# Fused attention block on one core: TensorE multiplies zeros at the start and between the last steps, and the planner's opening times move forward

## The chip, the cores and the metric

The kernel runs on one core of a Trainium2 chip. The time is the device time in microseconds of one launch. The core's engines run side by side, each in the order of its own program: TensorE (PE in the rows, with PEld for its weight loads), VectorE (DVE), ScalarE (ACT), GpSimd (POOL) and SyncE (SP, which here issues most DMAs). They wait for each other by semaphores. TensorE's clock has two levels, 1.2 and 2.4 GHz; the profile calls the upper one 1.00 and the lower one 0.50.

## The reference, cut to what matters

One transformer block, post-norm, for 2048 tokens of width 128, 16 heads of 8, all in fp32:

```
qkv  = x @ W_qkv.T                      # 2048 x 384
q, k = rope(q), rope(k)
p    = softmax(causal(q @ k.T / sqrt(8)))
attn = (p @ v) @ W_o.T
x1   = layernorm(x + attn)
w    = int4_simulated(kernel)           # scale = max|kernel| / 7, round, clip
out  = layernorm(x1 + x1 @ w + bias + (x1 @ a) @ b)
```

## The kernel before, in words

The 2048 tokens are cut into four chunks of 512, the 16 heads into four groups of four. A task is one group on the queries of one chunk; causality means that chunk c needs the keys of chunks 0 to c. `ORDER` lists the sixteen pairs, the last one is split into two halves, so that there are 17 tasks, 0 to 16. Tasks 15 and 16 hold two tiles of 128 tokens each, the others four.

For each task TensorE does three kinds of work. "A" units are scores with queries on the partitions, of which VectorE takes row maxima (L1231 with its masks L1241 and L1245 on TensorE, L1052 on VectorE). "M" turns the maxima into rows (L1255), VectorE splits them in two parts (L1072, L1074), and GpSimd's DMAs put them beside the queries (L890), so that the maximum is subtracted inside the second product. "S" steps are the scores again, with keys on the partitions (L1275), ScalarE takes the exponentials (L974), GpSimd zeroes the upper triangle on diagonal blocks (L881). "PV" steps multiply by the values and by a column of ones (L1289), into one PSUM bank a task; ScalarE copies that bank out (L983), "O" transposes it to rows of tokens (L1298), VectorE divides by the sums (L1098, L1100).

Behind the last group of a chunk come its "POST" steps: 2 transposes the attention's output (L1315), ScalarE or VectorE copies it; 3 multiplies by W_o (L1317), VectorE adds x and takes the statistics (L1125, L1128, L1131); RSTD is on GpSimd (L853, L856), NORM on VectorE (L1140), BIAS on GpSimd (L861); 4 transposes again (L1319); 5 multiplies by the quantised weights (L1321); then statistics, RSTD and NORM once more, and the store. For the last three tasks ScalarE copies the results of 2 and 4 (L988).

The opening is a fixed list, `PROLOGUE`: P projects a chunk for q (0) or k (1), plain and with swapped pairs (L1199), into one of four banks in turn; VectorE multiplies by the cosine and sine table `cs` (L1022; for chunks 2 and 3 ScalarE copies and GpSimd multiplies, L897); R adds the two (L799, on VectorE for chunk 0, on GpSimd for the rest); H is ScalarE's rounding to the high part (L951), T the low part (L804, same engine as R); E selects the rows of group 0 by a multiply with a 0/1 matrix (L1215) and copies them; D stores the parts to DRAM; X transposes x of a chunk (L1188), V projects the values (L1205). Before that list TensorE transposes two weight blocks (L1174) and x of chunk 0 (L1188, copied by VectorE at L1013). GpSimd's program starts with memsets and casts (L808 to L848) and has its R and T steps behind them.

What sets the order of all this is a planner that runs when the kernel is built (`Course`, `schedule()`): a beam search over a model of the engines, with rough costs. Its clock starts at `BEGIN`, entries of `PROLOGUE` with a first number are not taken before that time, `IN_DRAM` says when each chunk's parts are in DRAM and the loads of later operands can begin, and the low-rank step L is due at a fixed 200.0. These numbers reach the chip only through the order that comes out, `SCHEDULE`: every engine walks the same list and issues its own part, with waits on semaphores, not on times. The planner also deals out the eight PSUM banks: `take` picks one, `give` says when it is free again, `HELD` keeps which event had which. The bank of a task's PV sums is given back when ScalarE has copied it out.

In that list the TensorE steps after O of task 16, the last task, are POST 2 of 16, 4 of 15, 3 of 16, 5 of 15, 4 of 16, 5 of 16; on VectorE the statistics of POST 5 of task 15 stand ahead of NORM 0 of task 16.

## Time and profile before

| | us |
|---|---|
| three runs | 441.98, 443.64, 443.79; median 443.64 |
| the profiled execution | 442.17 |
| its span (first to last instruction) | 440.4 |
| TensorE busy | 415.8 (94%) |
| VectorE busy | 379.3 (86%) |
| ScalarE busy | 317.4 (72%) |
| GpSimd busy | 119.3 (27%) |
| mean granted clock of TensorE | 0.984 |

A row of a timeline is: start in the span, duration, engine, line, operation, what is written and read, shape, how many instructions are merged, and in brackets how long the engine had been idle and what ended that. An fp32 multiply leaves two records on TensorE, a transpose one. A duration of several merged records runs from the first start to the last end, the drain of the last included, so that the next instruction on TensorE can begin before it is over. The column of the granted clock shows 1.00 until the trace has its first event of the clock.

### The profile page before, as it was taken

How to read it: one execution, taken by the hardware profiler on the slowest of the kernel's cores; microseconds unless marked ns; L12 is line 12 of the kernel's file. 1: busy time of each engine (PE TensorE's matmuls, PEld its weight loads, DVE VectorE, ACT ScalarE, POOL GpSimd, SP SyncE). 2: the span in 40 equal slices, each digit the busy share in tenths (PEclk: the TensorE clock that was granted, in tenths of full speed). 3: DMA queues.
4: the chain of work that ended last, by engine and by line, in shares of the span. 5: the costliest groups of instructions: out<-in, count | busy, mean ns of one | idle time of the engine just before them, and what ended most of it. 6: DMA issues, size and time to landing. Idle time of an engine off the chain costs nothing.

```text
span 440.4 us, 8586 instructions
## 1 busy us (share of the span) xinstructions
PE 415.8 (94%) x3246; PEld 205.3 (47%) x3246; DVE 379.3 (86%) x491; ACT 317.4 (72%) x643; POOL 119.3 (27%) x188
## 2 busy tenths in 40 slices
PE   5989899799999999999999999999999999999982
PEld 2546445344436353455443644444354454435651
DVE  2878799899999999999999999999987988585585
ACT  2454884386975687777888788878788878898760
POOL 8979602102113100223110322011003012225463
PEclk9999999799999999999999999999999999999996
DMA  7522322210000000022200022200000000000001
GB/s 241 177 97 90 111 81 71 56 30 3 2 0 2 4 1 3 1 80 63 61 3 0 2 66 77 60 3 0 2 1 2 1 3 2 3 25 2 1 26 48
DMA packets 12201, 16.58 MB, mean 38 GB/s; under 512 B 2444, under 2 KB 7324, under 8 KB 12160
## 3 DMA queue, kind: packets, MB, share of 16 engines
q1 hardware_dynamic: 11072, 15.75, 11.3%
q8 instruction: 26, 0.43, 0.4%
q0 software_dynamic: 1088, 0.28, 0.4%
q14 instruction: 15, 0.12, 0.1%
HBM read 10.37 MB, written 5.24 MB: 35 GB/s over the span
## 4 chain that ended last, share of the span: by engine, by line
PE 81%; DVE 8%; ACT 5%; issue 3%; POOL 1%; DMA 1%; POOLq 0%; DVEq 0%; ACTq 0%
PE ps L1289 28%; PE ps L1275 23%; PE ps L1231 17%; DVE pmax L1052 7%; ACT probs L974 4%; PE ps L1199 3%; PE ps L1298 2%; PE ps L1245 1%; PE ps L1241 1%; PE ps L1205 1%; PE ps L1255 1%; PE ps L1317 1%; POOL rstd L856 1%; PE ps L1215 1%; DMA wqkv_sb<-in_L_attn_W_qkv_dram 1%
## 5 line engine op out<-in xcount | busy, mean ns | idle before, releaser
L1052 DVE TENSOR_REDUCE pmax<-ps 128x2 f32<-128x1024 f32 (+3 forms) x273 | 319.2, 1216 | 34.5 <-PE ps L1231 18.7
L974 ACT ACTIVATE probs<-ps 128x512 f32<-128x512 f32 (+2 forms) x576 | 285.4, 583 | 78.1 <-PE ps L1275 76.6
L1275 PE MATMUL ps<-qS,kS 64*128 64x512 f32 (+3 forms) x664 | 163.8, 404 | 2.7 <-DVE pmax L1052 1.3
L1231 PE MATMUL ps<-kS,qS 64*128 64x512 f32 (+3 forms) x640 | 141.9, 414 | 5.5 <-DVE pmax L1052 2.4
L1289 PE MATMUL ps<-probs,vP 128*9 128x512 f32 (+3 forms) x1328 | 144.3, 520 | 0.2
L1275 PEld LDWEIGHTS ps<-qS,kS 64*128 64x128 f32 x664 | 84.5, 186 | 85.5 <-ACT probs L974 61.4
L1231 PEld LDWEIGHTS ps<-kS,qS 64*128 64x128 f32 x640 | 67.1, 185 | 59.8 <-DVE pmax L1052 28.6
L881 POOL TENSOR_SCALAR_AFFINE_SELECT probs<-probs 128x512 f32<-128x512 f32 x64 | 40.3, 635 | 109.7 <-ACT probs L974 109.6
L890 POOL DMA_DIRECT2D qS<-mrows x34 | 19.6, 578 | 167.6 <-DVE mrows L1072 167.4
L1289 PEld LDWEIGHTS ps<-probs,vP 128*9 128x9 f32 x1328 | 22.2, 89 | 42.2 <-issue 24.4
L1245 PEld LDWEIGHTS ps<-causal_x,ident_x 64*128 64x128 f32 x188 | 19.1, 186 | 0.0
L1245 PE MATMUL ps<-causal_x,ident_x 64*128 64x256 f32 (+1 forms) x188 | 18.8, 248 | 0.0
L1241 PEld LDWEIGHTS ps<-causal_x,ident_x 64*128 64x128 f32 x136 | 15.3, 185 | 1.2
L983 ACT COPY oT<-ps 128x512 f32<-128x512 f32 (+1 forms) x17 | 9.6, 566 | 6.2 <-PE ps L1289 6.1
L1241 PE MATMUL ps<-causal_x,ident_x 64*128 64x128 f32 (+1 forms) x136 | 13.0, 230 | 0.0
L1199 PE MATMUL ps<-xT,wT 128*128 128x512 f32 x16 | 9.8, 699 | 1.6 <-DVE xT L1013 0.9
L1298 PE MATMUL ps<-ident,oT 128*128 128x128 f32 x64 | 10.7, 287 | 0.6 <-ACT oT L983 0.6
L897 POOL TENSOR_TENSOR rot<-rot,cs 128x512 f32<-128x512 f32 x8 | 10.1, 1282 | 2.9 <-ACT rot L921 2.9
L856 POOL TENSOR_TENSOR rstd<-rstd,mhalf 128x4 f32<-128x4 f32 (+1 forms) x10 | 9.2, 924 | 0.8
L1298 PEld LDWEIGHTS ps<-ident,oT 128*128 128x128 f32 x64 | 6.7, 141 | 5.3 <-issue 2.8
L1199 PE MATMUL ps<-xT,wTs 128*128 128x512 f32 x16 | 9.1, 651 | 0.0
L1022 DVE TENSOR_TENSOR rot<-ps,cs 128x512 f32<-128x512 f32 x8 | 5.3, 687 | 3.5 <-PE ps L1199 3.4
(116 smaller groups left out, 196.1 us busy)
## 6 DMA issues: line engine op xcount, KB each, us to landing
qS<-q_parts SPq DMA_DIRECT2D x52, 64.0 KB
kS<-k_parts SPq DMA_DIRECT2D x52, 64.0 KB
cs<-rope_tables_dram SPq DMA_DIRECT2D x4, 512.0 KB, 6.5
q_parts<-qp SPq DMA_DIRECT2D x4, 512.0 KB, 2.9
k_parts<-kp SPq DMA_DIRECT2D x4, 512.0 KB, 2.8
x_sb<-in_L_attn_x_dram SPq DMA_DIRECT2D x4, 256.0 KB, 5.7
out_dram<-rot SPq DMA_DIRECT2D x2, 256.0 KB, 2.3
qS<-mrows POOLq DMA_DIRECT2D x30, 8.0 KB, 1.8
```

The costliest lines, as they stand in the source:

```text
L856: nc.gpsimd.tensor_tensor(rstd[i][:, first:end], rstd[i][:, first:end], mhalf[:, first:end], ALU.pow).then_inc(pool_post[n], 1)
L881: pool.affine_select(out=p, in_=p, compare_op=ALU.is_ge, fill=0.0, base=0, pattern=[[0, HG], [1, TOK]], channel_multiplier=-1).then_inc(ma ...
L890: pool.dma_start(qS[at:at + 2 * SHIFT_STEP + 1:2 * SHIFT_STEP, b, c, :, lo:hi].bitcast(fp32), mrows[0:count, n % 2, a, 0:w].bitcast(fp32)) ...
L974: nc.scalar.activation(probs[:, J % PRING, heads[0]:heads[-1] + 1:2, lo:hi], bank_of(("S", n, j, i))[:, 0:len(heads) * (hi - lo)].rearrang ...
L1052: nc.vector.tensor_reduce(dst, src, AX.X, ALU.max).then_inc(unit_free, 1)
L1199: nc.tensor.matmul(bank, weights, xT[:, c, :], start=True, stop=True).then_inc(bank_done[prep_bank_of((kind, c))[0]], 1)
L1231: last = nc.tensor.matmul(ps[:, HELD[e][hl], at:at + w], qS[rows, b, c, hp, ii * TOK:(ii + 1) * TOK], kS[rows, b, kk, hp, 0:w], start=i == ...
L1241: last = nc.tensor.matmul(ps[:, HELD[e][hl], at + lo:at + TOK], ident_x[rows, x, :], causal_x[rows, x, 0, lo:], start=False, stop=upper == 1)
L1245: last = nc.tensor.matmul(tiles[:, first:first + step // TOK + 1:step // TOK, lo:], ident_x[rows, x, :], causal_x[rows, x, :, lo:], start= ...
L1275: last = nc.tensor.matmul(bank_of(("S", n, j, i))[:, x * w:(x + 1) * w], kS[rows, b, j // TPC, hp, (j % TPC) * TOK:(j % TPC + 1) * TOK], q ...
L1289: last = nc.tensor.matmul(bank_of(("PV", n, 0))[VW * h:VW * h + VC, lo:hi], vP[:, j, HG * g + h, :], probs[:, J % PRING, h, lo:hi], start= ...
L1298: last = nc.tensor.transpose(bank_of(e)[:, t * TOK:(t + 1) * TOK], oT[:, n % 2, t * TOK:(t + 1) * TOK], ident[:, :])
```

## The change

TensorE gets a helper `fill(count, bank)`: so many multiplies of a 128x128 block of zeros by itself, fp32, into 128 columns of a PSUM bank that nobody reads then. GpSimd writes the zeros as its first memset, TensorE waits for it. There are five fills before the wait for the weights, one between the weights' transposes and those of x of chunk 0, two after the latter (all into bank 0), and five after each POST step that comes behind O of the last task, into the bank of that task's PV sums; for that the planner does not give this bank back. The planner's times of the opening are smaller by 2.2 from the first that isn't 0, and by 2.0 for `IN_DRAM`.

```
--- before.py
+++ after.py
@@ -128,12 +128,12 @@
 PROLOGUE = ((0, 0, "P", 0, 0), (0, 0, "R", 0, 0), (0, 0, "H", 0, 0), (0, 0, "P", 0, 1), (0, 0, "T", 0, 0), (0, 0, "X", 1), (0, 0, "R", 0, 1),
             (0, 0, "H", 0, 1), (0, 0, "T", 0, 1), (0, 0, "P", 1, 0), (0, 0, "R", 1, 0), (0, 0, "E", 0, 0), (0, 0, "E", 0, 1), (0, 0, "P", 1, 1),
             (0, 0, "R", 1, 1), (0, 0, "X", 2), (0, 0, "H", 1, 0), (0, 0, "T", 1, 0), (0, 0, "D", 0), (0, 0, "H", 1, 1), (0, 0, "T", 1, 1),
-            (21.5, 1.9, "P", 2, 0), (21.5, 0, "R", 2, 0), (24.8, 0.9, "E", 1, 0), (25.8, 0.9, "E", 1, 1), (26.0, 0, "D", 1),
-            (28.0, 1.9, "P", 2, 1), (28.0, 0, "R", 2, 1), (28.0, 0.6, "X", 3), (29.0, 0, "H", 2, 0), (29.0, 0, "T", 2, 0),
-            (31.0, 1.9, "P", 3, 0), (31.0, 0, "R", 3, 0), (31.0, 1.1, "V", 0), (33.0, 0, "H", 2, 1), (33.0, 0, "T", 2, 1),
-            (35.0, 1.9, "P", 3, 1), (35.0, 0, "R", 3, 1), (35.0, 1.1, "V", 1), (36.0, 0, "D", 2), (37.0, 1.1, "V", 2), (40.0, 1.1, "V", 3),
-            (44.0, 0.9, "E", 2, 0), (45.0, 0.9, "E", 2, 1), (45.0, 0, "H", 3, 0), (45.0, 0, "T", 3, 0), (48.0, 0, "H", 3, 1),
-            (48.0, 0, "T", 3, 1), (48.0, 0, "D", 3))
+            (19.3, 1.9, "P", 2, 0), (19.3, 0, "R", 2, 0), (22.6, 0.9, "E", 1, 0), (23.6, 0.9, "E", 1, 1), (23.8, 0, "D", 1),
+            (25.8, 1.9, "P", 2, 1), (25.8, 0, "R", 2, 1), (25.8, 0.6, "X", 3), (26.8, 0, "H", 2, 0), (26.8, 0, "T", 2, 0),
+            (28.8, 1.9, "P", 3, 0), (28.8, 0, "R", 3, 0), (28.8, 1.1, "V", 0), (30.8, 0, "H", 2, 1), (30.8, 0, "T", 2, 1),
+            (32.8, 1.9, "P", 3, 1), (32.8, 0, "R", 3, 1), (32.8, 1.1, "V", 1), (33.8, 0, "D", 2), (34.8, 1.1, "V", 2), (37.8, 1.1, "V", 3),
+            (41.8, 0.9, "E", 2, 0), (42.8, 0.9, "E", 2, 1), (42.8, 0, "H", 3, 0), (42.8, 0, "T", 3, 0), (45.8, 0, "H", 3, 1),
+            (45.8, 0, "T", 3, 1), (45.8, 0, "D", 3))
 
 COPIED = 2
 
@@ -161,7 +161,7 @@
 PICKED = 3
 LOADED = list(dict.fromkeys((g, x) for g, c in ORDER for x in range(c, -1, -1) if g > 0 or x >= PICKED))
 
-IN_DRAM = (22.0, 30.0, 50.0, 62.0)
+IN_DRAM = (20.0, 28.0, 48.0, 60.0)
 PIECE, LOAD_PIECES, LANDED = 0.9, 8, 2.0
 
 
@@ -350,7 +350,8 @@
             self.probs = self.probs[:i] + (end + 0.15,) + self.probs[i + 1:]
             if j == steps(n) - 1:
                 self.act = max(self.act, end + 0.25) + 0.6
-                self.give(self.act + self.TO_PE, self.sums)
+                if n < len(TASKS) - 1:
+                    self.give(self.act + self.TO_PE, self.sums)
                 self.due += ((self.act + self.TO_PE, "O", n),)
         elif kind == "M":
             self.aside(0.25, 0.6, ready)
@@ -477,7 +478,7 @@
 
 HELD = {}
 FAR = 1e9
-BEGIN = 20.5
+BEGIN = 18.3
 WIDTH, WEIGHTS = 200, (1.0, 2.0, 1.0)
 SCHEDULE = schedule()
 RING_EVENTS = ("A", "M", "L", "O", "POST")
@@ -525,6 +526,7 @@
         b_sb = sb("b_sb", [RANK, D])
         bias_sb = sb("bias_sb", [128, D])
         ident = sb("ident", [128, 128])
+        zeros = sb("zeros", [128, 128])
 
 
         mask_raw = sb("mask_raw", [128, 2, 2, 128])
@@ -586,6 +588,7 @@
         ld_x = [sem(f"ld_x{c}") for c in range(NC)]
         ld_cs = [sem(f"ld_cs{c}") for c in range(NC)]
         consts = sem("consts")
+        zeros_set = sem("zeros_set")
         mask_set = sem("mask_set")
         q_filled = sem("q_filled")
         k_filled = sem("k_filled")
@@ -805,6 +808,7 @@
 
         @block.gpsimd
         def _(pool):
+            pool.memset(zeros[:, :], 0.0).then_inc(zeros_set, 1)
             pool.memset(ident[:, :], 0.0).then_inc(consts, 1)
             pool.wait_ge(consts, 1)
             pool.affine_select(out=ident[:, :], in_=ident[:, :], compare_op=ALU.not_equal, fill=1.0, base=0,
@@ -1167,12 +1171,20 @@
 
         @block.tensor
         def _(pe):
+            def fill(count, bank=0):
+
+                for _ in range(count):
+                    nc.tensor.matmul(ps[:, bank, 0:TOK], zeros[:, :], zeros[:, :], start=True, stop=True)
+
+            pe.wait_ge(zeros_set, 1)
+            fill(5)
             pe.wait_ge(consts, 2)
             pe.wait_ge(ld_w, 16)
             bank = prep_begin(pe, ("W", 0))
             for w in range(2):
                 last = nc.tensor.transpose(bank[:, w * 128:(w + 1) * 128], wqkv_sb[:, w, :], ident[:, :])
             last.then_inc(bank_done[0], 1)
+            fill(1)
 
             def side_weights():
                 pe.wait_ge(ld_side, 32)
@@ -1189,6 +1201,7 @@
                 last.then_inc(bank_done[prep_bank_of(("X", c))[0]], 1)
 
             transpose_x(0)
+            fill(2)
 
             def project(c, w):
                 if c == 0:
@@ -1346,6 +1359,8 @@
                     values(*e[1:])
                 if e[0] == "POST":
                     post(*e[1:])
+                    if SCHEDULE.index(e) > SCHEDULE.index(("O", len(TASKS) - 1)):
+                        fill(5, HELD["PV", len(TASKS) - 1, 0][0])
 
 
 _INS = ['L0_attn_x', 'L0_attn_W_qkv', 'L0_attn_W_o', 'L0_ffn_kernel', 'L0_ffn_bias', 'L0_ffn_a', 'L0_ffn_b']
```

## Rows read from the trace of the kernel before

**Rows 1.** The page: busy shares, slices, chain by engine

```profile
PE 415.8 (94%) x3246; PEld 205.3 (47%) x3246; DVE 379.3 (86%) x491; ACT 317.4 (72%) x643; POOL 119.3 (27%) x188
...
PEclk9999999799999999999999999999999999999996
...
PE 81%; DVE 8%; ACT 5%; issue 3%; POOL 1%; DMA 1%; POOLq 0%; DVEq 0%; ACTq 0%
```

**Rows 2.** Windows: stretch, busy by engine (instructions), PEclk, DMA share, GB/s; the middle

```profile
82.00:84.00 2.00, 1.68 (x7) 0.95 (x6) 2.00 (x3) 1.54 (x3) 0.00 (x0) 0.50 0.29 82
...
88.00:90.00 2.00, 1.92 (x10) 0.99 (x6) 1.85 (x2) 2.00 (x5) 0.00 (x0) 0.85 0.25 66
```

**Rows 3.** Timeline of the opening, 0 to 14 us

```profile
0.79 0.20 POOL L808 MEMSET ident<- 128x128 f32 x1 [0.29 <-POOLq L1361]
...
3.67 0.66 PE L1174 MATMUL ps<-ident,wqkv_sb 128*128 128x128 f32 x2 [3.67 <-DMA wqkv_sb<-in_L_attn_W_qkv_dram]
...
4.34 1.12 PE L1188 MATMUL ps<-ident,x_sb 128*128 128x128 f32 x4
...
5.49 0.69 DVE L1013 COPY xT<-ps 128x512 f32<-128x512 f32 x1 [3.53 <-PE ps L1188]
...
6.33 2.05 PE L1199 MATMUL ps<-xT,wT 128*128 128x512 f32 x2 [0.88 <-DVE xT L1013]
...
9.88 1.14 PE L1199 MATMUL ps<-xT,wT 128*128 128x512 f32 x2
...
11.71 0.27 PE L1180 MATMUL ps<-ident,wqkv_sb 128*128 128x128 f32 x1
...
13.31 1.13 PE L1199 MATMUL ps<-xT,wT 128*128 128x512 f32 x2 [0.67 <-ACT xT L921]
```

**Rows 4.** The DMA of the first table, L735, issued at 1.81: time to landing

```profile
DMA to landing us min/median/max: 5.7/5.7/5.7
```

**Rows 5.** Timeline, 14 to 36 us: GpSimd's queue and the row selection

```profile
18.11 1.26 POOL L799 TENSOR_TENSOR rot<-rot 128x512 f32<-128x512 f32 x1
...
18.40 1.48 DVE L1022 TENSOR_TENSOR rot<-ps,cs 128x512 f32<-128x512 f32 x2 [0.18 <-PE ps L1199]
...
20.02 1.28 POOL L799 TENSOR_TENSOR rot<-rot 128x512 f32<-128x512 f32 x1 [0.64 <-issue]
...
21.25 1.28 POOL L804 TENSOR_TENSOR qp<-rot,qp 128x512 fp32r<-128x512 f32 x1
...
23.64 1.20 PE L1215 MATMUL ps<-qp,pick 128*128 128x512 f32 x4
```

**Rows 6.** The chain of waits: four value projections of 128 columns (start, us)

```profile
38.86 1.09 PE ps L1205 x8
```

**Rows 7.** Timeline of the tail, 420 to 441 us

```profile
428.14 0.41 PE L1315 MATMUL ps<-ident,on 128*128 128x128 f32 x2 [0.68 <-DVE on L1100]
...
428.39 0.38 PE L1319 MATMUL ps<-ident,cs 128*128 128x128 f32 x2
...
429.11 0.68 PE L1317 MATMUL ps<-wT,cs 128*128 128x128 f32 x4 [0.33 <-ACT cs L988]
...
429.63 0.61 PE L1321 MATMUL ps<-ffn_q,cs 128*128 128x128 f32 x4
...
430.94 0.42 DVE L1125 TENSOR_TENSOR cs<-ps,cs 128x256 f32<-128x256 f32 x1
...
432.16 0.60 DVE L1140 TENSOR_SCALAR cs<-cs,mv,rstd 128x128 f32<-128x128 f32 x2
...
432.91 0.41 PE L1319 MATMUL ps<-ident,cs 128*128 128x128 f32 x2 [2.67 <-DVE cs L1140]
...
433.83 1.20 PE L1321 MATMUL ps<-ffn_q,cs 128*128 128x128 f32 x4 [0.51 <-issue]
...
435.06 0.42 DVE L1125 TENSOR_TENSOR cs<-ps,cs 128x256 f32<-128x256 f32 x1 [0.69 <-PE ps L1321]
```

**Rows 8.** Windows: the microsecond in which the clock falls

```profile
433.00:434.00 1.00, 0.49 (x3) 0.28 (x4) 0.63 (x1) 0.37 (x1) 1.00 (x2) 0.68 0.00 0
```

More of the change, by code:

```diff
@@ L162 @@
 LOADED = list(dict.fromkeys((g, x) for g, c in ORDER for x in range(c, -1, -1) if g > 0 or x >= PICKED))
-IN_DRAM = (22.0, 30.0, 50.0, 62.0)
+IN_DRAM = (20.0, 28.0, 48.0, 60.0)
 PIECE, LOAD_PIECES, LANDED = 0.9, 8, 2.0
@@ L352, in take @@
                 self.act = max(self.act, end + 0.25) + 0.6
-                self.give(self.act + self.TO_PE, self.sums)
+                if n < len(TASKS) - 1:
+                    self.give(self.act + self.TO_PE, self.sums)
                 self.due += ((self.act + self.TO_PE, "O", n),)
@@ L479 @@
 FAR = 1e9
-BEGIN = 20.5
+BEGIN = 18.3
 WIDTH, WEIGHTS = 200, (1.0, 2.0, 1.0)
@@ L527, in attention_block @@
         ident = sb("ident", [128, 128])
+        zeros = sb("zeros", [128, 128])
         mask_raw = sb("mask_raw", [128, 2, 2, 128])
@@ L588, in attention_block @@
         consts = sem("consts")
+        zeros_set = sem("zeros_set")
         mask_set = sem("mask_set")
@@ L807, in _ @@
         def _(pool):
+            pool.memset(zeros[:, :], 0.0).then_inc(zeros_set, 1)
             pool.memset(ident[:, :], 0.0).then_inc(consts, 1)
@@ L1169, in _, with fill @@
         def _(pe):
+            def fill(count, bank=0):
+                for _ in range(count):
+                    nc.tensor.matmul(ps[:, bank, 0:TOK], zeros[:, :], zeros[:, :], start=True, stop=True)
+            pe.wait_ge(zeros_set, 1)
+            fill(5)
             pe.wait_ge(consts, 2)
@@ L1175, in _ @@
             last.then_inc(bank_done[0], 1)
+            fill(1)
             def side_weights():
@@ L1191, in _ @@
             transpose_x(0)
+            fill(2)
             def project(c, w):
@@ L1348, in _ @@
                     post(*e[1:])
+                    if SCHEDULE.index(e) > SCHEDULE.index(("O", len(TASKS) - 1)):
+                        fill(5, HELD["PV", len(TASKS) - 1, 0][0])
 _INS = ['L0_attn_x', 'L0_attn_W_qkv', 'L0_attn_W_o', 'L0_ffn_kernel', 'L0_ffn_bias', 'L0_ffn_a', 'L0_ffn_b']
```

12 rows, old and new, of the table PROLOGUE are left out of this document.

## The prediction

> **What bounds the kernel now.** I read the page's busy shares and slices first, then the chain of waits, then the timeline of the opening and of the tail, because the diff touches only those two ends. The reader is to see that TensorE (PE) is busy for 94% of the span and carries 81% of the chain [rows 1]: a microsecond taken from TensorE early arrives at the end almost whole, unless another engine's queue holds the same stretch. The granted clock in the slices is full but for two places, a dip in the middle and the last slice. The dip is at half clock (1.2 of 2.4 GHz) from about 82 to about 88 us [rows 2]; nothing in the diff aims at it.
>
> In the opening the clock column says 1.00 throughout, but the durations say otherwise. The Q projections of chunk 0 begin at 6.33, the K projections at 9.88 and the transposes behind them at 11.71 [rows 3]: the same two multiplies by 512 columns took 3.55 us and then 1.83 us, so TensorE ran at half clock until about 9.9 and at full clock behind it. Half of 3.55 is the prize: 1.78 us. Before it the weight transposes wait for their DMA until 3.67, and there is a gap of 0.88 us before 6.33, which ends with VectorE's copy of xT [rows 3]. In the tail the clock falls at about 433.3 (mean 0.68 in that microsecond) after TensorE had stood idle from 430.24 to 432.91 [rows 7, 8], and only the very last multiply, POST 5 of task 16, is hit: 1.20 us [rows 7] where two such multiplies took 0.52 us from start to start (429.11 to 429.63) and 0.61 with their drain [rows 7]. The prize in the tail is 0.6 us.
>
> **The opening, step by step.** The memset of zeros goes ahead of GpSimd's (POOL's) first of ident. The one of ident, the same 128x128, took 0.20 us [rows 3]: every setup step of GpSimd comes 0.2 us later. Ident is still ready long before 3.67, so TensorE loses nothing by that.
>
> The price of one filling multiply (128x128, fp32, 128 columns): eight records, four multiplies of the same shape, take 1.09 us in the chain [rows 6], 0.27 each; POST 3 gives 0.26 [rows 7]. From below, a quarter of a 512-column projection at full clock is 1.83/2/4 = 0.23. I take 0.26 at full clock, and twice the lower one, 0.46, at half clock. Five before the weights land: 2.3 us, from about 1.1 (zeros written at 0.99) to about 3.4, inside the wait for the DMA: nothing, at most 0.1 us if the start is late. One between the weight transposes and those of x: it starts at about 4.15 and ends at about 4.6, while x's transposes began at 4.34: they and the xT copy behind them come 0.27 us later. Two after x's transposes: 0.92 us from about 5.5 to 6.45; the projections then start at 6.6 (6.33 + 0.27) anyway, so these two are covered by VectorE's copy.
>
> What they buy: TensorE is then occupied nearly without a hole from 1.1 to 6.6. In the trace of before the clock was low through broken work (the wait until 3.67, the gap before 6.33) and for 3.55 us more; with the holes filled I take it to be full when the projections start. Four 512-column multiplies then take 2 x 1.83 = 3.66 us from 6.6, the end is 10.25 instead of 11.71: 1.45 us earlier. Operands allow it: the table cs of chunk 0 is issued at 1.81 and lands 5.7 us later, at 7.5 [rows 4], and VectorE needs it first at 6.6 + 0.9. The next link, the projections of chunk 1 at 13.31 [rows 3], hangs on the chain rotation, high part, copies on ScalarE, which starts from the Q projections, and so shifts by about the same (Q's own end comes 1.5 us earlier).
>
> Then comes a cap, GpSimd. It is never idle in its fixed setup until 18.1, and this moves 0.2 later, not earlier. Its sum for chunk 1's q starts right behind it (18.11, 1.26 long), the one for k waits at 20.02 for VectorE's rotation, over at 19.88 [rows 5]. With everything else 1.5 us earlier the k sum is held by GpSimd itself: 18.31 + 1.26 = 19.6, only 0.4 before 20.02. The low part for q behind it (21.25, 1.28 long) then ends at 22.1, and the row selection on TensorE, now at 23.64, can begin at 22.15: 1.45 us earlier at most [rows 5]. So of whatever TensorE wins before, 1.45 us passes here, measured against this execution. I take 1.4 us for the opening. Bounds: from 0.3 lost (the clock rises when it did, and only the delay of 0.27 stays) to 1.45 won.
>
> The moved times (first 21.5 to 19.3, BEGIN 20.5 to 18.3, all by 2.2; arrivals in DRAM by 2.0) change no instruction. They shift the planner's clock, and a plan whose inputs all shift alike stays the same. Two do not: the arrivals (0.2 later relative to the rest) and the fixed due time 200.0 of the low-rank step; and the last task's sum bank is no longer handed back. So the order in the middle may come out slightly different. I price that at 0, with bounds of 1.5 us to each side; that is no more than the 1.8 us by which runs of one and the same order differ (441.98 to 443.79).
>
> **The tail, step by step.** After the transposes O of task 16, TensorE has six POST steps: 2 of task 16 at 428.14, 4 of task 15 at 428.39, 3 of task 16 at 429.11, 5 of task 15 at 429.63, 4 of task 16 at 432.91, 5 of task 16 at 433.83 [rows 7]. The change puts five fills, 5 x 0.26 = 1.3 us, behind each, and TensorE takes them in order, whether anything real is ready or not. The gaps between the first four are far shorter than that.
> POST 2 (16) starts 428.14, leaves TensorE at 428.39; fills to 429.69. POST 4 (15), 0.25, to 429.94; fills to 431.24. POST 3 (16) starts 431.24 instead of 429.11: 2.1 late, and this is the step that the end hangs on. It takes 0.52; fills to 433.06. POST 5 (15) 433.06 instead of 429.63. On VectorE the statistics of that step stand ahead of NORM 0 of task 16: they begin 0.73 us after it (433.79), and NORM starts 1.22 us after their beginning (432.16 against 430.94) [rows 7], so at 435.0 instead of 432.16. POST 4 (16) follows 0.75 later at 435.76 (fills end at 434.88, no wait). It takes 0.25, its fills end at 437.31; the copy on ScalarE would have let POST 5 (16) go 0.92 later, at 436.68, so 0.63 more is lost. At full clock it is over 0.61 later, and VectorE's add starts at 437.95 instead of 435.06: 2.9 us later, the saved 0.6 included. Behind it nothing changes, and the last fills end before the output is out. With fills of 0.22 each the same steps give 2.1, with 0.27 they give 3.1 (four blocks of fills stand on the path).
>
> **A rule against the change.** A transpose on TensorE here writes no other mark on the clock than any multiply: the rows show only that 1.8 us of transposes from 3.67 did not bring it up, nor keep it from being low at 6.33 [rows 3]. The Trainium skill ("TensorE: Matmul & The Clock Gate", Part 4, PE-mode transpose) says that transposes do not keep the clock gate open in the way that multiplies do; no row here separates that from the gap. By that rule the fills alone would have to carry the stretch, and the time is that of the first rival, 446.8; without it, 444.4.
>
> **The sum.** 442.17 (span 440.4 and 1.8 around it) - 1.4 + 2.9 = 443.7 us for the execution that was profiled. It is a quick one: the median of the runs is 443.64, 1.5 above it, the lowest 441.98. I don't know whether the slower executions lose that 1.5 in the opening, where the fills would win it back, or in the dip, where they would not; half of it is added: 444.4 us.
>
> **Rivals.**
> (a) The clock comes no sooner: the holes before 3.67 and the transposes count as idleness. Then the opening costs 0.3 and the tail 2.9: 442.17 + 3.2 = 445.4, or 446.8 on the median. It decides from the point where the Q projections still take over 3 us. For it: the transposes of before brought no rise. Against: with the fills TensorE is occupied nearly throughout.
> (b) The tail costs little, because the planner, which no longer gets the sum bank back, puts POST 3 (16) ahead of POST 4 (15), or because fills of zeros run faster than real data. One block of fills less in front, 1.3, leaves 1.6: 442.4, or 443.1 with the half; with both, and all of the 1.5 won back, 441. Against it: the bank is not scarce there.
> (c) The new order in the middle avoids or shortens the half-clock stretch of 82 to 88 us: some 6.4 us at half clock are worth up to 3.2, less as VectorE is full there [rows 2]; I take 2: 442.4. It can as well get a second such stretch: 446.4.
>
> **Chances.** Forecast 0.50, (a) 0.20, (b) 0.13, (c) 0.17, shared between its signs. The clearly slower side, over 0.5% (which is about what a measurement of this kernel can tell from no change, 2.2 us, so above 445.9): most of (a), half of (c) and the upper edge of the forecast, 0.24. Below 441.4: parts of (b) and (c), 0.08. Between: 0.68. Range 441.9 to 446.9; the forecast's own, from the tail's 2.1 to 3.1 and the median's 0 to 1.5, is 442.9 to 445.4.
>
> **What will show it.** Q's projections at 6.6, chunk 0's four done by 10.3 (right), or after 11.7 (a). The row selection of chunk 1 at about 22.2, with GpSimd's low part just ended. In the tail POST 3 (16) some 2.1 later behind O (16) than now, POST 5 (16) some 10.2 us after O (16) instead of 6.8, at full clock. The forecast is wrong if that distance grows by under 1.5 us, or if the middle, 24 to 427, changes its length by more than 1.5.

## The result, and the profile after

| | before | changed |
|---|---|---|
| first measurement, median | 443.01 us (4 runs, 441.98 to 443.79) | 447.85 us (4 runs, 445.84 to 448.83) |
| ratio, 95% interval | | 1.0105 (1.0057 to 1.0153) |
| measured again beside other kernels, median | 443.79 us | 446.31 us (12 runs, 445.84 to 448.08) |
| ratio, 95% interval | | 1.0061 (1.0031 to 1.0091) |
| profiled execution, its span | 442.17, 440.4 | 445.84, 444.1 |

The change makes the kernel slower, by 1.05% in the first measurement and by 0.61% in the second, larger one. The forecast was 444.4 with a range up to 446.9 and 0.68 on "within 0.5%": it missed the first median by 3.5 us and the upper end of the range by 1 (the second median, 446.31, lies inside); the side that came was given 0.24. Two executions of 540 us at a mean granted clock of 0.65, one of the sixth and one of the seventh kernel below, are left out of their ratios, but not of their medians.

First the page of the changed kernel, the answers to [rows 1]: TensorE is busier (its 76 new records are the fills), and the last two slices are both at 8 tenths instead of at 9 and 6.

```profile
PE 424.8 (96%) x3322; PEld 214.9 (48%) x3322; DVE 378.9 (85%) x491; ACT 317.1 (71%) x643; POOL 119.8 (27%) x189
...
PEclk9999999699999999999999999999999999999988
...
PE 78%; DVE 7%; POOL 5%; ACT 5%; issue 4%; POOLq 0%; DVEq 0%; ACTq 0%
```

Then its timeline, TensorE in the opening (start, us, engine, line, operation), against [rows 3]:

```profile
1.04 2.51 PE L1177 MATMUL ps<-zeros 128*128 128x128 f32 x10 [1.04 <-POOL zeros L811]
...
3.49 0.66 PE L1185 MATMUL ps<-ident,wqkv_sb 128*128 128x128 f32 x2
...
3.94 0.64 PE L1177 MATMUL ps<-zeros 128*128 128x128 f32 x2
...
4.54 0.81 PE L1200 MATMUL ps<-ident,x_sb 128*128 128x128 f32 x4
...
5.20 0.61 PE L1177 MATMUL ps<-zeros 128*128 128x128 f32 x4
...
6.23 1.10 PE L1212 MATMUL ps<-xT,wT 128*128 128x512 f32 x2 [0.43 <-DVE xT L1017]
...
9.74 0.27 PE L1192 MATMUL ps<-ident,wqkv_sb 128*128 128x128 f32 x1
```

The projections start at 6.23 at full clock and end at 9.74 instead of 11.71. Already the transposes of x are quick (0.81 against 1.12). Further on, GpSimd is the cap that the prediction named: the low part for q runs from 20.70 to 22.00, and the row selection waits for it until 22.26 (23.64 before, [rows 5]):

```profile
18.25 2.51 POOL L802 TENSOR_TENSOR rot<-rot 128x512 f32<-128x512 f32 x2
...
20.70 1.30 POOL L807 TENSOR_TENSOR qp<-rot,qp 128x512 fp32r<-128x512 f32 x1
...
22.26 1.15 PE L1228 MATMUL ps<-qp,pick 128*128 128x512 f32 x4 [0.44 <-POOL qp L807]
...
26.25 0.73 PE L1244 MATMUL ps<-kS,qS 64*128 64x512 f32 x4 [1.15 <-ACT kS L970]
```

The last of these, the first unit of task 1, began at 27.86 before: 1.61 us won. (It is one execution; how often the eight fills did this is said with the eleventh kernel.) The tail of the changed kernel, TensorE and the VectorE row that matters, against [rows 7]:

```profile
426.63 0.41 PE L1311 MATMUL ps<-ident,oT 128*128 128x128 f32 x2 [0.58 <-ACT oT L987]
...
426.95 1.11 DVE L1144 TENSOR_SCALAR rot<-rot,mv,rstd 128x128 f32<-128x128 f32 x4 [1.73 <-POOL rstd L860]
427.98 0.20 DVE L1102 RECIPROCAL rsum<-ps 128x8 f32<-128x8 f32 x1
...
428.58 0.66 PE L1328 MATMUL ps<-ident,on 128*128 128x128 f32 x2 [1.54 <-DVE on L1104]
429.03 2.34 PE L1177 MATMUL ps<-zeros 128*128 128x128 f32 x10
...
431.17 0.59 PE L1332 MATMUL ps<-ident,cs 128*128 128x128 f32 x2
431.59 1.28 PE L1177 MATMUL ps<-zeros 128*128 128x128 f32 x10
...
432.71 0.61 PE L1330 MATMUL ps<-wT,cs 128*128 128x128 f32 x4
...
434.27 0.61 PE L1334 MATMUL ps<-ffn_q,cs 128*128 128x128 f32 x4
...
436.72 0.41 PE L1332 MATMUL ps<-ident,cs 128*128 128x128 f32 x2 [0.72 <-DVE cs L1144]
...
438.08 0.61 PE L1334 MATMUL ps<-ffn_q,cs 128*128 128x128 f32 x4
```

O of task 16 is only 0.42 us earlier than before (427.05), so 1.19 of the 1.61 are lost in between. All of that lies behind O of task 12, which comes at 375.37 (376.98 before, 1.61 earlier). From O to the start of the last POST 5 it is 11.45 us instead of 6.78; that step ends 0.6 sooner by its clock. Together: -1.61 + 1.19 + 4.67 - 0.59 = 3.66, and the spans differ by 3.7. A window over the tail shows the first block of fills at about half clock, which is why it takes 2.14 us from start to start and each of the others 1.12:

```profile
428.00:430.00 2.00, 1.42 (x7) 1.45 (x8) 0.91 (x5) 0.37 (x1) 0.72 (x1) 0.54 0.46 131
430.00:432.00 2.00, 2.00 (x13) 2.00 (x13) 0.00 (x0) 0.21 (x1) 0.00 (x0) 0.60 0.00 0
432.00:434.00 2.00, 2.00 (x20) 2.00 (x20) 0.61 (x2) 0.17 (x1) 0.00 (x0) 1.00 0.00 0
```

VectorE's rows show another cause: NORM 1 of task 14 (426.95) now stands ahead of O of task 16, and POST 2 of task 16 follows O by 1.95 us instead of 1.09. That is order, not fills.

### The profile page after: what moved, and what is told of

The parts are those of the page before. It is cut to its first block, busy times and chain, and to the rows that moved or that the text cites. A ratio compares the mean times of both kernels' runs of the same rounds, so it can differ in the third digit from the quotient of the medians.

```text
span 444.1 us, 8742 instructions
## 1 busy us (share of the span) xinstructions
PE 424.8 (96%) x3322; PEld 214.9 (48%) x3322; DVE 378.9 (85%) x491; ACT 317.1 (71%) x643; POOL 119.8 (27%) x189
## 4 chain that ended last, share of the span: by engine, by line
PE 78%; DVE 7%; POOL 5%; ACT 5%; issue 4%; POOLq 0%; DVEq 0%; ACTq 0%
PE ps L1302 29%; PE ps L1288 23%; PE ps L1244 17%; DVE pmax L1056 6%; ACT probs L978 4%; PE ps L1311 2%; PE ps L1212 1%; PE ps L1258 1%; PE ps L1218 1%; PE ps L1254 1%; PE ps L1330 1%; POOL kS L851 1%; PE ps L1334 1%; POOL qS L852 1%; PE ps L1268 1%
## 5 line engine op out<-in xcount | busy, mean ns | idle before, releaser
L1258 PE MATMUL ps<-causal_x,ident_x 64*128 64x128 f32 (+1 forms) x188 | 18.7, 248 | 0.0
L1177 PE MATMUL ps<-zeros 128*128 128x128 f32 x76 | 12.5, 320 | 1.0 <-POOL zeros L811 1.0
L1254 PE MATMUL ps<-causal_x,ident_x 64*128 64x64 f32 (+1 forms) x136 | 12.6, 231 | 0.0
L1177 PEld LDWEIGHTS ps<-zeros 128*128 128x128 f32 x76 | 11.6, 234 | 1.0 <-POOL zeros L811 1.0
L1311 PE MATMUL ps<-ident,oT 128*128 128x128 f32 x64 | 10.6, 286 | 0.6 <-ACT oT L987 0.6
L1212 PE MATMUL ps<-xT,wT 128*128 128x512 f32 x16 | 8.8, 630 | 1.1 <-ACT xT L925 0.7
```

The costliest lines, as they stand in the source:

```text
L1177: nc.tensor.matmul(ps[:, bank, 0:TOK], zeros[:, :], zeros[:, :], start=True, stop=True)
L1212: nc.tensor.matmul(bank, weights, xT[:, c, :], start=True, stop=True).then_inc(bank_done[prep_bank_of((kind, c))[0]], 1)
L1254: last = nc.tensor.matmul(ps[:, HELD[e][hl], at + lo:at + TOK], ident_x[rows, x, :], causal_x[rows, x, 0, lo:], start=False, stop=upper == 1)
L1258: last = nc.tensor.matmul(tiles[:, first:first + step // TOK + 1:step // TOK, lo:], ident_x[rows, x, :], causal_x[rows, x, :, lo:], start= ...
L1311: last = nc.tensor.transpose(bank_of(e)[:, t * TOK:(t + 1) * TOK], oT[:, n % 2, t * TOK:(t + 1) * TOK], ident[:, :])
```

## The experiments

Why did the order change? What changes it is the fixed due time 200.0 of the low-rank step, which is 2.2 us later against all that moved. With 197.8 in its place the changed kernel has the old order step for step; the lists part at a unit of task 8, two entries ahead of L. Arrivals moved by 2.2 like the rest instead of 2.0, or the bank given back, leave the changed kernel's list as it is. (Started from the kernel before, the new arrivals, the new `BEGIN` or the new `PROLOGUE` by itself gives a list that parts within the first hundred entries: it is the joint shift that keeps the order.) The bank that is kept changes no order, only the banks of a few late POST steps. So the change has three separable parts, and the first four kernels take them one by one.

### The opening's fills alone

```
-                self.due += ((200.0, "L"),)
+                self.due += ((197.8, "L"),)
...
-                    if SCHEDULE.index(e) > SCHEDULE.index(("O", len(TASKS) - 1)):
-                        fill(5, HELD["PV", len(TASKS) - 1, 0][0])
```

> The changed kernel without the five fills behind the late POST steps, and with the low-rank step due at 197.8 instead of 200.0, which gives every engine exactly the order of the kernel before: only the opening's fills (and the memset of zeros) are left. Theory A (costs add up: opening, order, tail): 1.6 us faster than the kernel before, because the first units of task 1 began at 26.25 instead of 27.86 and everything behind them shifts; projections of chunk 0 from 6.2 to 9.8, O of task 16 near 425.4. Rival B (the opening's gain is absorbed in the middle, where TensorE catches up with VectorE or the loads): within 0.4 us of the kernel before, with O of task 16 at about 427. Rival C (multiplies of zeros cost clock later): slower, mean granted clock under 0.98.

Measured: 440.99 us against 443.37, ratio 0.9952 (0.9929 to 0.9974). O of task 16 is at 425.56. Theory A; B falls, and so does C: it is not slower, and its granted clock is under 0.98 in seven of twelve executions, about as often as before (16 of 32). In its trace the projections run from 6.43 to 10.41, not from 6.2 to 9.8: the clock came up within the first of them, and the first unit of task 1 is at 26.47, 0.2 later than expected.

### The order alone

Against the kernel before:

```
-                self.due += ((200.0, "L"),)
+                self.due += ((202.2, "L"),)
```

> The kernel before with one number changed: the low-rank step due at 202.2 instead of 200.0. Without any fill this gives exactly the order of the changed kernel, from task 8 on. Theory A: 1.2 us lost in the middle (the stretch from the first units of task 1 to O of task 16 grew from 399.2 to 400.4) and 0.9 us between O of task 16 and its POST 2, because NORM 1 of task 14 now stands ahead of O of task 16 on VectorE: 2.1 us slower. Rival B (order is neutral, the opening's gain was absorbed in the middle): within 0.5 us. If the order also costs clock in some executions, its timed runs are over 2.1 slower while the profile shows 2.

Measured: 445.30 us against 443.37, ratio 1.0052 (1.0030 to 1.0074). One number in a planner, and no fill, costs as much as the opening's fills win. Its timeline at the end:

```profile
427.30 0.41 PE L1289 MATMUL ps<-probs,vP 128*9 128x128 f32 x8 [0.73 <-POOL probs L881]
428.30 0.41 PE L1298 MATMUL ps<-ident,oT 128*128 128x128 f32 x2 [0.58 <-ACT oT L983]
430.25 0.66 PE L1315 MATMUL ps<-ident,on 128*128 128x128 f32 x2 [1.54 <-DVE on L1100]
430.76 0.66 PE L1319 MATMUL ps<-ident,cs 128*128 128x128 f32 x2
```

The loss is not spread over the middle. O of task 12 is at 377.04 here and was at 376.98; O of task 16 is at 428.30 and was at 427.05: 1.25 us lost in the last four tasks. 0.73 of that is a wait that was not there, for GpSimd's mask of the last diagonal block; the rest I can't pin to one step. The loss is no chance of this execution: from O of task 12 to O of task 16 it is 51.2 to 51.3 us in all five traces with the new order and 50.1 in all nine with the old one. Then 0.86 more until POST 2, behind NORM 1 of task 14, and TensorE runs at half clock from there on (0.66 us for two transposes), which makes the whole span 3.1 us longer (443.5 against 440.4).

### The tail's fills alone

```
-            fill(5)
...
-            fill(1)
...
-            fill(2)
...
-                self.due += ((200.0, "L"),)
+                self.due += ((197.8, "L"),)
```

> The changed kernel without the eight fills of the opening and with the low-rank step due at 197.8, so the order of the kernel before: only the fills behind the six late POST steps are left. With the fill measured at 0.244 us in the changed kernel (1.22 for five) the steps of the prediction give 4 x 1.22 - 2.31 = 2.6 us slower; theory A adds up to 1 us if the first block falls into half clock (it took 2.34 there), but in this order POST 2 follows O by 1.1 and not 1.95 us, so the clock should stay up: 2.6. Rival B (all of the 4.1 us between O and the last POST 5 are fills): 4.1 slower.

Measured: 446.51 us against 443.37, ratio 1.0069 (1.0038 to 1.0099), so 3.1 us with 1.7 to 4.4. In its trace the last POST 5 starts 9.18 us after O of task 16, against 6.78 before; less the 0.59 saved by the clock this is 1.8 us. The trace decides against B (4.1) and lies under A's 2.6; the interval of the runs holds all three. Two things in the profiled execution's time stand ahead of the fills and were not caused by them: a half-clock stretch from about 50 to beyond 56 us, and an opening in which, with no fills in it, the projections end at 13.31 and the first unit of task 1 begins at 29.25 (11.71 and 27.86 in the execution of the kernel before).

### All fills, the old order

```
-                self.due += ((200.0, "L"),)
+                self.due += ((197.8, "L"),)
```

> The changed kernel with the low-rank step due at 197.8 instead of 200.0: all fills stay, the order is that of the kernel before. Theory A: -1.6 and +2.6 make 1.0 us slower than the kernel before, 2.7 us faster than the changed kernel's profiled execution (445.84). Rival B: like the changed kernel, 3.7 us slower than before.

Measured: 444.28 us against 443.37 in the medians, ratio 0.9997 (0.9971 to 1.0022): no difference that can be told: 0.1 us faster by the ratio, 0.9 slower by the medians, where A said 1.0 slower. B falls. Its tail (timeline):

```profile
427.03 0.41 PE L1311 MATMUL ps<-ident,oT 128*128 128x128 f32 x2 [0.58 <-ACT oT L987]
428.13 0.41 PE L1328 MATMUL ps<-ident,on 128*128 128x128 f32 x2 [0.69 <-DVE on L1104]
428.38 1.28 PE L1177 MATMUL ps<-zeros 128*128 128x128 f32 x10
...
430.83 0.61 PE L1330 MATMUL ps<-wT,cs 128*128 128x128 f32 x4
...
436.20 0.61 PE L1334 MATMUL ps<-ffn_q,cs 128*128 128x128 f32 x4
```

POST 3 of task 16 starts 3.80 after O (2.06 before), and every block is at full clock (1.12 us from start to start). In this execution O of task 16 is not early at all although the opening was: the windows of the same trace show the clock down at 48 us, where the kernel before had it up.

```profile
48.00:50.00 2.00, 2.00 (x10) 1.26 (x9) 1.57 (x4) 1.37 (x3) 1.59 (x3) 0.50 0.73 266
50.00:52.00 2.00, 2.00 (x12) 1.90 (x12) 2.00 (x3) 2.00 (x6) 1.43 (x2) 0.50 0.18 57
52.00:54.00 2.00, 2.00 (x12) 0.27 (x9) 1.52 (x2) 1.10 (x3) 1.27 (x2) 0.50 0.78 265
```

TensorE has idled before it: 1.2 us for ScalarE's kS and 0.5 for the first exponentials. That wait is in every kernel here that has no fills there, but the clock falls behind it in some executions only. What the fall costs can be read from the way between the first unit of task 1 and O of task 12: 350.6 to 350.9 us in the four traces in which it lasts as long as here (the third, fourth, eighth and ninth kernels), 349.1 in the kernel before. In the first kernel's trace it lasts half as long and costs nothing (349.0). The kernel before shows steps in its 32 executions of this comparison: granted clock 0.980 goes with a span near 440.9, 0.976 with 442.4, 0.972 with 443.4.

### Fills in those waits

The order here, and in all that follow but for the eighth to the tenth kernel, is that of the kernel before (197.8).

```
+                if n == 2 and unit == units(2)[0]:
+                    banks_taken(pe, e)
+                    fill(5, HELD[e][0])
...
+                if e in (("A", 3, ("keys", 1, 2, 0)), ("A", 3, ("keys", 1, 2, 1))):
+                    bank = HELD["M", 2][0]
+                    pe.wait_ge(*RELEASE["M", 2])
+                    fill(4 if e[2][3] == 0 else 2, bank)
...
-                    if SCHEDULE.index(e) > SCHEDULE.index(("O", len(TASKS) - 1)):
-                        fill(5, HELD["PV", len(TASKS) - 1, 0][0])
+                    if e[1:] == (len(TASKS) - 2, 5):
+                        fill(8, HELD["PV", len(TASKS) - 1, 0][0])
```

> Fills only where TensorE waits anyway, in the order of the kernel before: the opening's eight; five ahead of the first A unit of task 2, which waits 1.2 us for ScalarE's kS, into the bank that the unit is about to write; four and two behind the A units (1,2,0) and (1,2,1) of task 3, where TensorE waits 1.1 and 0.6 us for VectorE, into the bank that the rows of task 2 have left; and eight behind POST 5 of task 15, ahead of a wait of 2.7 us. Theory D (what the runs of one kernel differ by is the clock, which falls in those waits, near 48 and 82 us, for one stretch or more): the half-clock stretches at 48 and 82 us are gone, the mean granted clock is over 0.985 in every execution, the last POST 5 takes 0.61 instead of 1.19 us, and the kernel is 3 to 4 us faster than the opening fills alone, 5 to 6 faster than before. Rival E (VectorE and ScalarE bound the stretches at 48 and 82 us, so the low clock there costs nothing): only the tail's 0.6 us on top of the opening fills, 2.7 faster than before.

Measured: 441.32 us against 443.79, ratio 0.9932 (0.9899 to 0.9965). That is 2.5 us by the medians and 3.0 by the ratio: rival E's 2.7, not theory D's 5 to 6. Of theory D's signs the profiled execution has two: near 48 us the clock is up, which says little by itself, as it is up there in seven of the twelve traces without fills in that wait; and the last POST 5 takes 0.68 us instead of 1.20. Near 82 the clock still falls, here for longer than before (back up only between 92 and 94), and once more from 147 to 151; five of the twelve executions have a granted clock under 0.985. The executions spread from 438.3 to 443.6: the shortest span, 436.5, is the one at 0.995, the longest, 441.8, is at 0.980. And the profiled one takes 352.1 us from the first unit of task 1 to O of task 12, 3.0 more than the kernel before. Both speak against rival E, for a low clock that costs time, but how much of it at 82 and how much at 147 is not told apart. These six fills don't prevent the fall: behind them VectorE's queue still makes TensorE wait at 79.7 and 80.8.

### One block, in the wait of the tail

```
-                    if SCHEDULE.index(e) > SCHEDULE.index(("O", len(TASKS) - 1)):
-                        fill(5, HELD["PV", len(TASKS) - 1, 0][0])
+                    if e[1:] == (len(TASKS) - 2, 5):
+                        fill(8, HELD["PV", len(TASKS) - 1, 0][0])
```

> The opening's fills and eight fills (1.95 us) behind POST 5 of task 15 alone, where TensorE waits 2.7 us; order of the kernel before. Every theory: 0.6 us faster than the opening fills alone (440.99), since the last POST 5 runs at full clock and nothing stands in front of a step: 440.4. If over 0.3 slower than that, fills cost something even in an idle stretch.

Measured: 441.99 us against 443.79, ratio 0.9948 (0.9920 to 0.9975), beside 0.9952 for the opening's fills alone: the two can't be told apart. The trace shows why nothing is gained: the clock falls just ahead of the eight fills, at about 428.2, so that they take 3.25 us instead of some 1.8 and run past the wait. POST 4 of task 16 starts 6.44 us behind O, 5.86 before; what the last POST 5 saves at full clock (0.68 instead of 1.20) is lost again. The trace of the twelfth kernel does the same, that of the fifth does not.

### Only the five ahead of the weights

```
-            fill(1)
...
-            fill(2)
```

> Of the opening's fills only the five ahead of the weights; not the one and the two between the first transposes. Order of the kernel before. If the five alone bring the clock up: projections of chunk 0 at full clock from 6.3, 2 us faster than before, like all eight. If the holes at 4.1 to 6.3 matter, or transposes do not count as work: the Q projections take over 3 us again, and the time is that of before. By the Trainium skill (TensorE: Matmul & The Clock Gate, Part 4, PE-mode transpose) it is the second.

Measured: 442.54 us against 443.79, ratio 0.9988 (0.9962 to 1.0013): no gain that can be told. The timeline shows why:

```profile
4.54 1.12 PE L1199 MATMUL ps<-ident,x_sb 128*128 128x128 f32 x4 [0.49 <-DMA x_sb<-in_L_attn_x_dram]
6.53 2.04 PE L1210 MATMUL ps<-xT,wT 128*128 128x512 f32 x2 [0.88 <-DVE xT L1017]
8.37 1.91 PE L1210 MATMUL ps<-xT,wTs 128*128 128x512 f32 x2
10.07 1.10 PE L1210 MATMUL ps<-xT,wT 128*128 128x512 f32 x2
```

The clock rises at about 10 again. The five alone do nothing; with the three between 4 and 6.3 added it comes up sooner. Whether those three would do without the five was not run. The result fits the rule of the Trainium skill on transposes ("TensorE: Matmul & The Clock Gate", Part 4, PE-mode transpose), and it fits the holes (0.49 and 0.88 us) as well: a kernel with holes and no transposes was not run.

### The changed kernel again

No edit.

> The changed kernel again, beside the others, for a narrower interval. Theory A (the parts add: opening -2.1, order +2.3, tail fills +3.1 as measured): 3.3 us slower than the kernel before, 446.7. If the parts add more than their sum (the order leaves a hole of 1.5 us ahead of POST 2 of task 16, the clock falls and the first fills run at half of it): 4.3 to 4.8 slower.

Measured: 446.31 us against 443.79, ratio 1.0061 (1.0031 to 1.0091), 2.7 us: the sum of the parts (3.3) is inside, "more than the sum" (4.3 to 4.8) is outside the interval. The traces show some 0.4 us of it: from O of task 16 on, the changed kernel is 4.1 us longer than the one before, where the order alone (second kernel) and the fills alone (third) cost 1.8 each.

### NORM 1 of task 14 put back behind O of task 16

```
+SCHEDULE.remove(("NORM", 14, 1))
+SCHEDULE.insert(SCHEDULE.index(("NORM", 15, 0)) + 1, ("NORM", 14, 1))
 RING_EVENTS = ("A", "M", "L", "O", "POST")
```

> The changed kernel with its own order but for one step: NORM 1 of task 14 goes on VectorE (and its store on SyncE) from ahead of O of task 16 to behind NORM 0 of task 15, as the kernel before had it. Theory F (the order costs at its end only: VectorE reaches O of task 16 late, TensorE stands idle for 1.5 us, its clock falls and the first block of fills takes 2.1 instead of 1.1 us): POST 2 of task 16 follows O of task 16 by 1.1 instead of 1.95 us, all six blocks of fills run at full clock, 1.9 us faster than the changed kernel, 444.4. Rival G (the order costs in the middle): no more than 0.9 faster. If NORM 1 of task 14 only moves its cost to a later step of the chain, 0.9 or less as well.

Measured: 446.05 us, ratio 1.0052 (1.0025 to 1.0079) against 1.0061: 0.3 us faster than the changed kernel where theory F said 1.9. Its 444.4 lies just under the interval (444.6 to 447.0), rival G's "no more than 0.9" came. Yet the tail of the trace does what theory F says:

```profile
428.48 0.41 PE L1313 MATMUL ps<-ident,oT 128*128 128x128 f32 x2 [0.58 <-ACT oT L989]
429.54 0.41 PE L1330 MATMUL ps<-ident,on 128*128 128x128 f32 x2 [0.65 <-DVE on L1106]
429.78 1.28 PE L1179 MATMUL ps<-zeros 128*128 128x128 f32 x10
...
437.60 0.61 PE L1336 MATMUL ps<-ffn_q,cs 128*128 128x128 f32 x4
```

POST 2 follows O by 1.06 us, the first block takes 1.12, and from O to the last POST 5 it is 9.12 us instead of 11.45. So the tail's 2.3 us are shown in one trace; that they arrive in the time is not. Executions at granted clock 0.988 have a span of 441.8 here and of 444.0 and 444.1 in the changed kernel, 2.2 less, but at 0.983 it is 444.7 and 444.8 here and 444.4 there. Ten of twelve executions are at 0.985 or lower here and six of twelve there. In the traced one the clock is down from 48 to 55 and from 79 to 89 us, and the way from the first unit of task 1 to O of task 12 is 350.9 us against 349.1 in the changed kernel's first trace. Whether that is chance stays open.

### The changed kernel without the tail's fills

```
-                    if SCHEDULE.index(e) > SCHEDULE.index(("O", len(TASKS) - 1)):
-                        fill(5, HELD["PV", len(TASKS) - 1, 0][0])
```

> The changed kernel without the fills of the tail: its opening, its order. If parts add: -2.1 + 2.3 = 0.2 slower than before, 443.8 to 444. If the new order's loss in the order-only kernel came from the phase of the clock rather than from the order, it is nearer to the opening's fills alone, 441 to 442.

Measured: 445.15 us against 443.52, ratio 1.0032 (1.0007 to 1.0057), 1.4 us slower where the parts add to 0.2 (0.04% with about 0.3 to each side): on the side of "the order costs", and rather more than the sum, with an interval that reaches it. That the loss came from the phase of the clock rather than from the order (441 to 442) falls.

### One fill a block instead of five

```
-                        fill(5, HELD["PV", len(TASKS) - 1, 0][0])
+                        fill(1, HELD["PV", len(TASKS) - 1, 0][0])
```

> All of the opening's fills, the order of the kernel before, and one fill instead of five behind each of the six late POST steps. One fill is 0.22 us: POST 3 of task 16 then starts about 0.2 later (2 x 0.22 less the 0.47 us of slack), POST 5 of task 15 0.4 later but VectorE is still busy with POST 3 then; the chain loses 0.2 or less. The clock falls as in the kernel before. So within 0.4 us of the opening's fills alone: 441.0 to 441.4, 2 us faster than before. If the cost of fills is not their length but something paid once a block, it is nearer to 444.3.

Measured: 442.23 us against 443.52, ratio 0.9950 (0.9924 to 0.9977), the same as with the opening's fills alone. The last POST 5 starts 6.78 us behind O of task 16, exactly as before: the tail's price is the length of the blocks.

This trace shows something else as well, the one case in which the opening's eight fills did not help:

```profile
5.29 1.12 PE L1200 MATMUL ps<-ident,x_sb 128*128 128x128 f32 x4 [0.68 <-DMA x_sb<-in_L_attn_x_dram]
...
7.28 2.05 PE L1212 MATMUL ps<-xT,wT 128*128 128x512 f32 x2
9.12 1.81 PE L1212 MATMUL ps<-xT,wTs 128*128 128x512 f32 x2
```

x came 0.75 us later than in the changed kernel (5.29 against 4.54), TensorE had a hole of 0.68 us, the Q projections took 3.49 us, and the first unit of task 1 began at 28.54. In the nine other traces with all eight fills it began at 26.25 to 26.73, in the four traces without all eight at 27.82 to 29.25.

### The opening, and the two waits at 46 us and in the tail

The fifth kernel without its fills near 78 us:

```
-                if e in (("A", 3, ("keys", 1, 2, 0)), ("A", 3, ("keys", 1, 2, 1))):
-                    bank = HELD["M", 2][0]
-                    pe.wait_ge(*RELEASE["M", 2])
-                    fill(4 if e[2][3] == 0 else 2, bank)
```

> Opening fills, the five ahead of the first A unit of task 2 and the eight behind POST 5 of task 15; not the six near 78 us. Order of the kernel before. The fills at 46 us took the fall near 48 us away, those near 78 us did not take the fall at 82 us away. Theory D: the executions with the lowest clock (0.961 and 0.972 before) are gone, median 1 us under the kernel with the opening and the gap of the tail alone: 440 to 441, 3 faster than before. If the six near 78 us had been what helped, 442.

Measured: 440.62 us against 443.52, ratio 0.9928 (0.9899 to 0.9957); its executions lie within 2.1 us and its granted clock is 0.984 or higher in each. It beats both kernels: 2.9 us under the one before, some 6 under the changed one. It is not told apart from the fifth (0.9932), so the six fills at 78 us are worth nothing that shows. By its interval it is not told apart from the sixth kernel (0.9948) or from the opening's fills alone (0.9952) either; what speaks for the fills at 46 us is that none of its executions is under 0.984, where six of the sixth kernel's eleven at the usual clock are. Its window at 48 us is at full clock, the one at 82 us at half:

```profile
48.00:50.00 2.00, 1.71 (x10) 1.04 (x10) 1.87 (x4) 1.79 (x4) 1.27 (x4) 1.00 0.52 194
...
82.00:84.00 2.00, 2.00 (x11) 1.20 (x13) 1.99 (x3) 2.00 (x5) 0.00 (x0) 0.50 0.32 90
```

Its tail shows the eight fills at half clock, too long for the wait:

```profile
425.84 0.41 PE L1314 MATMUL ps<-ident,oT 128*128 128x128 f32 x2 [0.58 <-ACT oT L987]
...
429.13 3.31 PE L1177 MATMUL ps<-zeros 128*128 128x128 f32 x16
432.28 0.38 PE L1335 MATMUL ps<-ident,cs 128*128 128x128 f32 x2
433.17 0.68 PE L1337 MATMUL ps<-ffn_q,cs 128*128 128x128 f32 x4 [0.51 <-issue]
```

So in this trace (span 439.3, 1.1 under the kernel before) the whole gain is that of the opening, where the first unit of task 1 begins 1.13 us sooner.

## Why the prediction was wrong, step by step

**The price of a fill** was close: 0.26 forecast, 0.224 measured (1.12 for five) at full clock; 0.46 at half clock forecast, 0.43 measured in the changed kernel's first block (2.14 for five).

**The opening was right** in mechanism and size: the five cost nothing; 1.4 us forecast, with a cap of 1.45 at GpSimd's queue (by its own rows, 23.64 less 22.15, 1.49); 1.38 at the row selection and, a little over the cap, 1.61 at the first unit of task 1; 0.48% in the paired runs (0.26 to 0.71%, 1.2 to 3.1 us). The wait for GpSimd stands in the trace (0.44 us). Rival (a) did not come in this execution, but it did in one of the ten traced with all eight fills, that of the eleventh kernel (Q projections 3.49 us, over the 3 us that it named): the fills make an early clock likely, not certain.

**The step that failed** is the one on the moved times: "So the order in the middle may come out slightly different. I price that at 0, with bounds of 1.5 us to each side". The two constants that didn't shift were named, and one of them, the due time of the low-rank step, changed the list from task 8 on. The order-only kernel puts the price at 0.52% (0.30 to 0.74%), 2.3 us: outside the bounds, though the lower end of the interval, 1.3, is not. With all fills in both kernels (eighth against fourth) it is 0.64%, with the opening's alone (tenth against first) 0.80%. In its trace it is 2.1 us until POST 2 of task 16, 1.25 in the last four tasks and 0.86 at one step of VectorE, and then 1.0 of the clock. The bounds were taken from how far the times of one order lie apart, and these say nothing about how far two orders lie apart. The forecast of the tail leaned on the same step: it took VectorE's order from the kernel before. For the profiled execution, 443.7 forecast and 445.84 measured, this is the account of the 2.1 us: 0.2 less in the opening, 1.2 more in the middle, 1.2 more in the tail. The forecast's own signs of failure missed it: the distance from O to the last POST 5 did grow (by 4.67 us, forecast 3.5), and the middle changed by 1.2, under the 1.5 that was set.

**The tail was right in mechanism and, with the old order, in size**: 2.9 us forecast; 4 x 1.12 - 2.31 = 2.2 by its own steps with the measured fill; 1.8 in the traces of the third and fourth kernels (the statistics begin 0.65 us behind POST 5 and NORM 1.08 behind those, where 0.73, which no row shown gives, and 1.22 were taken), 3.1 (1.7 to 4.4) in the runs of the third. In the changed kernel it was 4.1, because POST 2 came late and the clock fell in that hole: the forecast's "at full clock" failed for the first block, again through the order. Rival (b) did not come: the bank made no difference to the order. Rival (c) did not come as it was put: the new order neither avoided the stretch near 82 us (half clock from 80 to 87 here) nor brought a second one in the middle of the profiled execution; the second one, near 48 us, came in the eighth kernel, which is the same program, and in kernels of either order.

**The sum**: -1.4 + 2.9 + 0 was forecast. By the paired runs it is -2.1 + 2.3 + 3.1 = 3.3, and the changed kernel's are 2.7 and 4.7. How far the first median lies outside the range is in part luck: it rests on four executions, of which two, 448.80 and 448.83, had a granted clock of 0.975 and 0.973; the twelve of the second measurement give 446.31. Whether half of 1.5 us was right to add for the median stays open, because only a quick execution of the kernel before was traced. The traces show a loss of either kind, in the opening and in the middle: with no fills the first unit of task 1 can come 1.4 us later (third kernel), and a fall of the clock costs 1.5 to 1.8, near 48 us though and not in the dip at 82 that was named.

## What to carry to other kernels

Filling work has to stand where the engine waits anyway, and be shorter than the wait even if it runs at half clock: one block of five behind each step cost 0.69%, such multiplies in the waits of the opening, at 46 us and in the tail won 0.72%, of which the opening's alone give 0.48; the eight in the tail overran their wait at half clock in two traces of three and gained nothing there. When a planner orders a kernel, a shift of its times is only a shift if every constant moves; compare the order that comes out, engine by engine, before thinking about times, and give a new order its own wide bound. And look at what stands first in the queue behind the last task: there one swap on VectorE opened 0.9 us.

## What the runs showed of the hardware

Multiplies of zeros bring the clock up too: with eight of them the projections ran at full clock from 6.2, with none at half clock until 9.9. It is not the same in every execution: in nine of ten traces with the eight fills the clock was up within the first projection, in one only at about 10.6; without fills it came up at 9.9 and, in the third kernel's trace, after 12. The clock does not fall at every wait of one kind: behind the same 1.2 us near 46 us it stayed up in the profiled execution of the kernel before and fell in that of the fourth kernel. The span of one and the same kernel mostly goes by it: 0.980 with about 440.9 us, 0.972 with about 443.4.
